# Four chunks in step, or two halves of two: a new order of steps from the router on

## The reference

```python
h = _L0_tok_ref(x, ...)
h = h + _L0_attn_ref(_layernorm(h), ...)
h = h + _L0_ffn_ref(_layernorm(h), ...)    # softmax, top_k(probs, 2), 8 experts: gelu(xf @ w1 + bb1) @ w2 + bb2, weighted
h = h + _L1_attn_ref(_layernorm(h), ...)   # S = S*dec + sa*b + v*k per token; group norm; o * g @ W_o
h = h + _L1_ffn_ref(_layernorm(h), ...)    # relu(shared + routed + h), twice, then h @ Wo.T + bo
```

## Time and profile before

| | before |
|---|---|
| median of 3 runs | 394.02 us (389.51 to 397.53) |
| profiled execution | 395.19 us, its span 393.2 us |
| PE busy | 326.8 us, 83% |
| DVE busy | 220.6 us, 56% |
| ACT busy | 197.7 us, 50% |
| POOL busy | 142.3 us, 36% |
| mean granted clock of PE | 0.943 |

### The profile page before, as it was taken

How to read it: one execution, slowest core, us unless ns; L and a number is a source line. 1 busy time by engine, 2 the same in 40 slices (tenths; PEclk the granted TensorE clock), 3 DMA queues, 4 the chain that set the end, 5 groups by cost and what they waited for, 6 DMA issues and landing times.

```text
span 393.2 us, 13416 instructions
## 1 busy us (share of the span) xinstructions
PE 326.8 (83%) x5712; PEld 222.4 (57%) x5712; DVE 220.6 (56%) x446; ACT 197.7 (50%) x382; POOL 142.3 (36%) x146
## 2 busy tenths in 40 slices
PE   4999999999995999999677984597777799798465
PEld 2447876766862734343233544597776699345342
DVE  4567687787368632333595889965665303751002
ACT  1665465445454367677747794356000774646120
POOL 9009999512000055564243006699900000310000
PEclk9999999999997799999959998699999999879996
DMA  8622222110012221221000000000000000000002
GB/s 274 262 59 62 65 58 65 51 49 3 3 47 61 58 58 56 60 63 33 1 0 0 2 0 0 3 4 3 3 6 5 3 5 3 0 0 5 3 5 77
DMA packets 20563, 14.92 MB, mean 38 GB/s; under 512 B 2328, under 2 KB 19352, under 8 KB 20376
## 3 DMA queue, kind: packets, MB, share of 16 engines
q1 hardware_dynamic: 20504, 14.07, 11.5%
HBM read 13.32 MB, written 0.74 MB: 36 GB/s over the span
## 4 chain that ended last, share of the span: by engine, by line
PE 52%; DVE 17%; issue 12%; ACT 10%; POOL 8%; POOLq 0%; DVEq 0%
PE PS L785 48%; POOL arena L313 7%; PE PS L849 4%; DVE arena L588 2%; DVE arena L732 2%; DVE arena L571 2%; ACT arena L373 2%; ACT arena L370 1%; ACT arena L476 1%; ACT arena L485 1%; DVE PS L520 1%; ACT arena L489 1%; ACT arena L365 1%; DVE arena L735 1%; DVE arena L584 1%
## 5 line engine op out<-in xcount | busy, mean ns | idle before, releaser
L785 PE MATMUL PS<-arena,K 128*128 128x360 f32 (+2 forms) x576 | 149.7, 515 | 21.2 <-DVE arena L588 7.3
L785 PE MATMUL PS<-arena 128*45 128x45 f32 (+6 forms) x3648 | 118.5, 221 | 31.7 <-issue 15.4
L785 PEld LDWEIGHTS PS<-arena 128*45 128x45 f32 (+4 forms) x3648 | 100.7, 127 | 50.6 <-issue 36.4
L785 PEld LDWEIGHTS PS<-arena,K 128*128 128x128 f32 (+2 forms) x576 | 71.0, 183 | 81.8 <-issue 22.6
L313 POOL TENSOR_TENSOR arena<-arena 128x360 f32<-128x360 f32 x32 | 30.0, 948 | 68.8 <-DVE arena L694 68.2
L694 DVE TENSOR_TENSOR arena<-PS,arena 128x360 f32<-128x360 f32 x32 | 17.0, 533 | 33.7 <-ACT arena L419 33.7
L785 PE MATMUL PS<-K,arena 128*45 128x32 f32 (+4 forms) x768 | 26.1, 223 | 4.8 <-DVE arena L677 4.2
L785 PEld LDWEIGHTS PS<-K,arena 128*45 128x45 f32 (+2 forms) x768 | 25.3, 132 | 6.9 <-DVE arena L677 4.9
L397 ACT COPY arena<-PS 128x360 f32<-128x360 f32 x32 | 14.8, 467 | 24.5 <-PE PS L849 24.4
L415 ACT ACTIVATE arena<-PS,K 128x720 f32<-128x720 f32 x32 | 24.9, 861 | 2.5 <-PE PS L785 2.5
L341 POOL TENSOR_TENSOR arena<-arena 128x360 f32<-128x360 f32 x4 | 4.4, 1112 | 56.4 <-DVE arena L579 56.4
(11 more groups left out here) (126 smaller groups left out, 420.2 us busy)
## 6 DMA issues: line engine op xcount, KB each, us to landing
WG<-wr SPq DMA_DIRECT2D x64, 64.0 KB, 1.9
arena<-wr SPq DMA_DIRECT2D x64, 64.0 KB, 1.8
arena<-xT SPq DMA_DIRECT2D x4, 368.0 KB, 4.8
K<-consts SPq DMA_DIRECT2D x1, 1171.0 KB, 10.7
K<-consts SPq DMA_DIRECT2D x1, 852.0 KB, 10.4
out<-arena SPq DMA_DIRECT2D x4, 180.0 KB, 1.9
K<-consts SPq DMA_DIRECT2D x1, 510.0 KB, 8.3
K<-consts SPq DMA_DIRECT2D x1, 352.0 KB, 9.1
```

The lines of the kernel that those rows point to most:

```text
L785: return nc.tensor.matmul(o, l, r, start=start, stop=stop)
```

## The change

`schedule()` builds the same steps with helpers that take a set of chunks, `a` = chunks 0 and 1 and `b` = chunks 2 and 3. `ahead(x, y)` merges two lists: it puts steps of `y` between those of `x` in proportion to their lengths. Up to the router and for `hid 0`, `cwT`, `cw2` and `b2` the four chunks stay in step. From the first `y` on the order is in halves.

```diff
+    def after_attention(cs):
+        return (stage(cs, ("attT", 0), ("wo", 0)) + stage(cs, ("mean", 2)) + [stage(cs, ("var", 2))]
+                + stage(cs, ("gate", 0)) + [("top2", 0, a[0]), ("top2", 0, b[0])]
+                + [stage(cs, ("hid", 0))] + stage(cs, ("cwT", 0), ("cw2", 0), ("b2", 0)))
+    def experts(cs):
+        out = stage(cs, ("y", 0))
+        for i in range(1, E):
+            out += stage(cs, ("hid", i), ("y", i))
+        return out
+    def mix(cs):
+        out = stage(cs, ("mean", 3)) + [stage(cs, ("var", 3))]
+        for c in cs:
+            out += [("mixes", 0, c), ("rk", 0, c)]
+        return out + stage(cs, ("vw", 0))
...
+    order += after_attention(both_halves)
+    order += experts(a)
+    order += ahead(experts(b), mix(a))
+    order += ahead(mix(b), project(a))
+    order += ahead(invert(a), project(b))
+    order += ahead(invert(b), solve(a) + finish(a))
+    order += solve(b)
+    order += ahead(finish(b), routed(a))
+    order += routed(b)
```

`project` is `aw` to `kb`, `invert` is `m`, `vt` and the levels, `solve` is `u` to `o`, `finish` is norm 4 to `f`, `routed` is `r 0`, `r 1` and `fo`. Top-2 is done once for each half, on half as many elements:

```diff
-        def gate(r, n=C * PP * E):
+        def gate(c, r, n=C // 2 * PP * E):
...
-                    dve.wait_ge(sem["gate_mm"], C)
-                    steps = [0]
+                    dve.wait_ge(sem["gate_mm"], c + C // 2)
+                    steps = [TOP2_STEPS * (n - 1)]
...
-                        pe.wait_ge(sem["g_steps"], 1)
+                        pe.wait_ge(sem["g_steps"], TOP2_STEPS * (c // (C // 2)) + 1)
...
-                    if (i, c) == (PP // 2, 0):
+                    if (i, c) == (2, 0):
                         split_biases()
```

More of the change, by code:

```diff
@@ L78, with stage, norm, ahead @@
 LAG = 2
+TOP2_STEPS = 17
 def schedule():
[L83 to L96, removed]
+    halves_of_chunks = [range(0, C // 2), range(C // 2, C)]
+    def stage(cs, *steps):
+        return [(name, i, c) for name, i in steps for c in cs]
+    def norm(cs, k):
+        return stage(cs, ("mean", k), ("var", k))
+    def ahead(x, y):
+        out, taken = [], 0
+        for n, step in enumerate(x):
+            out.append(step)
+            while taken < len(y) and (taken + 1) * len(x) <= (n + 1) * len(y):
+                group = y[taken]
+                out += group if isinstance(group, list) else [group]
+                taken += 1
+        return out
[7 more added lines that the diff above has]
+            out += stage(cs, ("hid", i), ("y", i))
+        return out
+    def mix(cs):
[3 more added lines that the diff above has]
+        return out + stage(cs, ("vw", 0))
+    def project(cs):
+        return stage(cs, ("aw", 0), ("ab", 0), ("gh", 0), ("gg", 0), ("kk", 0), ("bon", 0), ("kb", 0))
+    def invert(cs):
+        out = stage(cs, ("m", 0), ("m", 1), ("vt", 0))
+        for i in range(len(LEVELS)):
+            out += stage(cs, ("lx", i), ("lt", i))
+        return out
+    def solve(cs):
+        return stage(cs, ("u", 0), ("y2", 0), ("z", 0), ("w", 0), ("o", 0))
+    def finish(cs):
+        return norm(cs, 4) + stage(cs, ("ro", 0)) + norm(cs, 5) + stage(cs, ("f", 0))
+    def routed(cs):
+        return stage(cs, ("r", 0), ("r", 1), ("fo", 0))
+    a, b = halves_of_chunks
+    both_halves = range(C)
+    order = stage(both_halves, ("tok", 0)) + norm(both_halves, 0) + norm(both_halves, 1)
+    order += stage(both_halves, ("q", 0), ("k", 0), ("v", 0), ("s", 0), ("e", 0))
@@ L106, in schedule @@
         if n >= LAG:
-            i, c = units[n - LAG]
-            order.append(("pv", i, c))
+            order.append(("pv",) + units[n - LAG])
         if 1 <= n <= len(units):
@@ L112, in schedule @@
                 order.append(("e", i + 1, c))
[L113 to L135, removed]
+    order += after_attention(both_halves)
[7 more added lines that the diff above has]
+    order += routed(b)
+    flat = []
+    for step in order:
+        flat += step if isinstance(step, list) else [step]
+    return flat
 ORDER = schedule()
@@ L404, in _ @@
                     act.wait_ge(sem["g_sub"], n)
-                    s.activation(gate(0), gate(0), ACT.Exp).then_inc(sem["g_exp"], 1)
+                    s.activation(gate(c, 0), gate(c, 0), ACT.Exp).then_inc(sem["g_exp"], 1)
                 elif name == "cwT":
@@ L893, in _ @@
                     if i == 0:
-                        pe.wait_ge(sem["cwT"], n)
-                        pe.wait_ge(sem["b2_add"], n)
-                    pe.wait_ge(sem["gelu"], n)
+                        pe.wait_ge(sem["cwT"], c + 1)
+                        pe.wait_ge(sem["b2_add"], c + 1)
+                    pe.wait_ge(sem["gelu"], COUNT["hid", i, c])
                     for j in range(2):
@@ L967, in _ @@
                 elif name == "lt":
-                    pe.wait_ge(sem["x_ev"], n)
+                    pe.wait_ge(sem["x_ev"], COUNT["lx", i, c])
                     for p in range(PP):
```

29 lines of the change are left out of this document (15 added, 14 removed).

## The result

The changed kernel takes 407.81 us (median of 4 runs, 406.99 to 408.56), the kernel before 393.91 in the same comparison: a ratio of 1.039, with an interval of 1.030 to 1.048. It is slower by 13.9 us, where 5 were forecast.

What follows compares the result with a forecast made beforehand. TensorE was taken as the bound, as an average (83% busy), with 55.3 us idle to win behind 118.7 us. Stretches summed to a span of 398.8, 400.8 with 2.0 around it; 1.2 over the median, so 399 us; range 384 to 412.

Steps and rivals of the forecast that it cites:

- Step 1: Top-2 in two halves, one behind the other on VectorE: experts start 2 us later, at 138.5.
- Step 2: Experts of half a with nothing interleaved, 4.05 us a step: 30.5 us, to 169.0.
- Step 3: Experts of b with the mix of a, norm and table loads put between: 43.3 us, to 212.3.
- the second rival: TensorE's clock stays low, decisive if the experts of b with a's mix run below about 0.8: 410 us; chance 0.20.
- Step 4: Mix of b with projections of a, ScalarE and VectorE alternating: 30.4 us, m of chunk 0 at 242.7.
- Step 5: Inversion of a with projections of b: 17.5 to the levels, levels 24, exposed kb of b 11.7; to 295.9.
- Step 6: Inversion of b with solve and finish of a, 43 us; then solve of b alone, 13.3; to 352.2.
- Step 7: Finish of b with routed layers of a, 22 us; routed layers and output of b, 20.6; to 394.8.
- Step 8: Three new bursts on the path starting at half clock rate, 1.3 us each: +4 us, span 398.8.
- The rule on table loads: Seven more ScalarE table loads: 9.0 us by the trace; with the skill's drain 18.6, the sum 9.7 higher.
- The first rival: Interleaved work fills TensorE's pauses in levels and routed layers and the clock never falls: 385 us; chance 0.24.
- Switches at twice their row: Rival: each ScalarE table switch costs at most as much again as its 1.28 us load: 408 us; chance 0.05.

Runs made afterwards that it cites:

- split_back: The changed kernel with split_biases back at attention step (4, 0) instead of (2, 0); 400.18 us, ratio 1.014 to the kernel before.
- experiments 1: Place of split_biases varied: changed kernel with it at (4, 0), 400.18 us, or (3, 0), 399.69 us; kernel before with it at (2, 0), 398.31 us.
- Experiment 3: split_back with the expert steps of all four chunks in step and halves only from mix on; 393.86 us, ratio 1.003 to the kernel before.
- experiment 4: split_back with all four chunks in step for longer: halves only from the levels on, 387.97 us, or only from the solve on, 392.71 us.
- experiment 2: split_back with norm 3's Ln and Exp and vw's tanh replaced by functions needing no load, 6 table loads instead of 12; 398.20 us.
- split_early: The kernel before with one edit alone, split_biases at (2, 0) instead of (4, 0); 398.31 us, ratio 1.011.

## Why the prediction came out as it did

The sign was right and the range held the time, but the forecast was 9 us low, on the near side of the 2%, and almost all of that is one term. The sum was 400.8 for the profiled execution; split_back's, without that term, took 401.27. (400.8 less 1.2 would be 399.6; the 399 on record is a rounding too low.) In medians the 13.9 us can be put together from runs: the place of the split +7.6, the experts in halves +6.3 (4.5 by the ratios), norm 3 to `vt` in halves +5.9, all behind it in halves -5.7 (experiments 1, 3 and 4), 14.1 in all. Point by point, against the changed kernel:

- **A line of the diff at no price.** The prediction said that everything ahead of 118.7 us stays. The move of `split_biases` was in the diff and got no term. The step that failed is the first: it took an unchanged order for an unchanged stretch. GpSimd's row in the same place would have shown where to ask: an 11.4 us run of `L290` from 62.37, into which the four instructions were moved. It cost 7.5 us; the profiled execution is 7.0 over the sum.
- **Step 1, top-2 in halves:** 2 charged, nothing measured. The experts start 6.7 us late (143.20 for 136.50), exactly as late as the attention ended. A step of 128 elements takes 0.29 us, not 0.35 to 0.43 (DVE, after):

```profile
129.86 0.29 DVE L702 TENSOR_TENSOR arena<-arena 128x128 f32<-128x128 f32 x1
```

- **Step 2, experts of a:** 30.5 charged, 30.3 measured, each step 4.04 us for 4.05 (the terms of the walk add up to 4.03). The round trip walked in the earlier trace rows was right.
- **Step 3, experts of b with the mix of a:** 43.3 charged, 46.3 measured (to the last copy, 219.8). The norm between two experts went as walked, only slower, 9.2 and 9.8 us from copy to copy for 9.3: ACT loads at 185.74, runs four functions, loads again, and comes to its gelu at 190.43:

```profile
185.74 1.28 ACT L385 ACT_TABLE_LOAD   x1
187.03 0.56 ACT L403 ACTIVATE arena<-PS,K 128x360 f32<-128x360 f32 x1
...
189.13 1.28 ACT L385 ACT_TABLE_LOAD   x1
190.43 1.61 ACT L448 ACTIVATE arena<-PS,K 128x720 f32<-128x720 f32 x2
```

  TensorE idles 3.50 us there and falls to the lower clock, as the second rival said, but only for one step, and once more for one group of `y` behind a wait of 2.44 us at 217.44:

```profile
191.34 1.47 PE L819 MATMUL PS<-arena,K 128*64 128x360 f32 x4 [3.50 <-ACT arena L448]
...
197.73 0.83 PE L819 MATMUL PS<-arena,K 128*64 128x360 f32 x4 [0.36 <-ACT arena L448]
```

  The clock of the stretch is 0.90, above the 0.8 from which that rival was to decide. Experiment 3 prices the halved experts in all at 7.2 us of span.
- **Step 4, mix of b with projections of a:** 30.4 charged, 31.1 measured.
- **Step 5:** `m` to the first level 17.2 (17.5); levels of a 25.2 (24). `kb` of b is as exposed as forecast: 11.7 us charged, 9.8 measured from 293.2 to 303, TensorE busy 4.86 at a clock of 0.65. The row in question, against the earlier trace rows:

```profile
297.96 4.78 PE L819 MATMUL PS<-arena 128*45 128x90 f32 x80 [4.82 <-ACT arena L498]
```

- **Step 6:** levels of b with solve and finish of a: TensorE is busy 43.6 of 45.5 us, so this is where the order does fill the pauses. From the first `m` to this stretch's end it is 97.6 us for 96.2 charged. This stretch is 2.5 over its own 43. The solve of b took 17.0 for 13.3, the largest miss of a priced term: TensorE waits for a copy of `u` on ACT (`L526`, at 352.92), which stands behind the last level's copies of both chunks (`L518`, `L522`) and the two `f` of a (`L542`), and then runs slow:

```profile
353.64 3.59 PE L819 MATMUL PS<-arena 128*45 128x64 f32 x64 [3.17 <-ACT arena L526]
```

- **Step 7:** 22.15 for 22, and 18.4 for 20.6.
- **Step 8, the clock:** 4 us in one sum, while the measured stretches hold theirs already. Steps 2 to 7 together are 6.6 us over their own terms (-0.2, +3.0, +0.7, -1.0, +6.2, -2.1), of which these 4 were to cover the clock; with step 1's 2 us not spent, all that was priced comes out 0.6 over. Sizes of both signs are in that, so the closeness is partly luck.
- **The rule on table loads:** seven loads more cost at most 9.0 us by the row's duration, and experiment 2 gave back 2 (medians) to 4 (trace) for six of them. The Trainium skill, "ScalarE: Activation LUTs", section "What ACT_TABLE_LOAD costs", adds a drain of about 1.38 us to each; the rows have no room for it here, neither behind a load (187.03 follows 185.74 by 1.29) nor ahead of it (the Exp at 188.61 takes 0.50, the load starts at 189.13).
- **The first rival, that the pauses fill (385):** the waits named "issue" did fall, by 13.2 us, but the time did not follow. Levels of a took 25.2 us where this rival had 21.5, the last stretch with finish of b 22.15 where it had 18: what was put into the pauses waits for round trips of its own, as was said against it. The pause of 1.08 us for each 128 passes that the prediction read from the earlier trace rows is the longest of them; in the levels of the kernel before they are 0.53 to 1.08. Without the thin pairs ahead of it the filling pays (experiment 4).
- **Switches at twice their row (408):** refuted by experiment 2, though its number is the one that came out. The low clock's 410 is near it too: a time that fits a rival says nothing for its mechanism.

Of the signs that were to show it right, four came: 4.04 us a step, a step of b over 8, the 4.82 us ahead of `m` of chunk 2, and fewer "issue" pauses. The fifth, `m` of chunk 0 at 240 to 247, missed at 250.88; without the split's delay it comes at 243.48 (split_back).

Left open: whether the cast in the changed kernel was let in because of the 0.19 us gap, which no run varied alone; and what makes the "issue" pauses and the clock give time back when the work ahead of them is late.

## What to carry to other kernels

Price every line of a diff, also one that lies in a stretch "that stays": look at what GpSimd does at the place to which a VectorE instruction moves, and for how long without a gap. Before you halve the number of chunks in step, compare a chunk's round trip with half the work of a step: in the experts it was 4.05 us against 3.34, and the halves lost there; they gained from the levels on, where TensorE already paused. Two routed layers beside a chain of round trips cost nothing here (20.3 us with them, 20.5 without), and the same two beside the solve, a short and busy stretch, cost 6.6.

## What the hardware showed that was not expected

- VectorE beside GpSimd: a cast of 0.28 us took 1.97 and 5.76, a 0.48 us instruction 4.09, each to the end of GpSimd's own. A cast that waited was not let in between two GpSimd instructions that followed without a gap (at 69.8, split_early), and it was where 0.19 us lay between (changed kernel).
- Small instructions are lengthened as well: in `kb`, 0.58 us became 1.36 beside a product of 0.94. Three products of 0.53 us on the same engine were cheaper than the same three beside it.
- One stall of 5.8 us on TensorE costs 1.7 more at the lower clock after it, and one of 3.50 some 1.6 in the two `y` groups behind it (twice 1.47 and 0.48 us, for 0.83 and 0.33 at full rate).
- Half of a late start (7.75 us in the attention) was gone at the end (3.6) though every engine does the same work in the same order; TensorE's "issue" pauses were 3.4 us shorter, and its clock fell at other places.
